# The causal mask moves from a fourth product of each diagonal tile into idle rows of its second and third product

## The reference

```
scores = einsum('bqhd,bkhd->bhqk', q_full, k_full) * softmax_scale
scores = where(causal, scores, finfo.min)      # key after query: hidden
attn   = softmax(scores)
out    = einsum('bhqk,bkhd->bqhd', attn, v)
```

## Time and profile before

| | |
|---|---|
| median of 3 runs | 773.95 us (773.89 to 774.18) |
| the profiled execution | 774.09 us |
| its span | 772.2 us |
| PE busy | 741.6 us, 96% of the span |
| DVE busy | 541.1 us, 70% |
| ACT busy | 326.4 us, 42% |
| POOL busy | 213.3 us, 28% |
| granted TensorE clock | 0.999 |

### The profile page before, as it was taken

The page is one execution under the profiler, slowest core; times in us unless marked ns, Lnnn a source line. Parts: engine busy times, 40 slices in busy tenths (PEclk is TensorE's granted clock), DMA queues, the critical chain, the costliest instruction groups (busy, mean ns, idle before and its releaser), DMA issues.

```text
span 772.2 us, 10622 instructions
## 1 busy us (share of the span) xinstructions
PE 741.6 (96%) x3931; PEld 513.4 (66%) x3931; DVE 541.1 (70%) x803; ACT 326.4 (42%) x499; POOL 213.3 (28%) x198
## 2 busy tenths in 40 slices
PE   3989999999999999999999999999999999999997
PEld 2856666666666666566566666555788888887886
DVE  6867678788788788888888889589695332123432
ACT  4834444545545545545545444444254322222210
POOL 1137624135235235235235211010255000000211
PEclk9999999999999999999999999999999999999999
DMA  8433523403303303303303390350201332200011
GB/s 312 173 76 88 125 56 83 90 9 83 92 8 83 91 8 83 90 10 83 87 12 82 71 346 21 111 191 28 57 26 28 97 79 70 75 11 1 28 42 41
DMA packets 36289, 60.73 MB, mean 79 GB/s; under 512 B 4272, under 2 KB 16560, under 8 KB 34448
## 3 DMA queue, kind: packets, MB, share of 16 engines
q1 hardware_dynamic: 36240, 60.06, 28.0%
HBM read 32.66 MB, written 2.10 MB: 45 GB/s over the span
## 4 chain that ended last, share of the span: by engine, by line
PE 70%; DVE 22%; issue 4%; ACT 2%; DMA 1%; POOL 0%; SPq 0%; DVEq 0%; ACTq 0%; POOLq 0%
PE PS L845 16%; PE PS L862 8%; PE PS L675 8%; DVE PR L1397 6%; PE PS L754 6%; PE PS L735 6%; PE PS L736 6%; PE PS L737 5%; PE PS L809 5%; DVE NMa L1305 4%; PE PS L666 3%; DVE NMd L1310 2%; PE PS L688 2%; PE PS L739 1%; DVE wide L1397 1%
## 5 line engine op out<-in xcount | busy, mean ns | idle before, releaser
L1053 ACT ACTIVATE PR<-PS 128x1024 f32<-128x1024 f32 (+1 forms) x144 | 133.1, 929 | 151.8 <-PE PS L737 127.4
L1305 DVE TENSOR_REDUCE NMa<-PS 128x1 f32<-128x512 f32 (+3 forms) x184 | 116.4, 656 | 34.7 <-PE PS L675 33.1
L675 PE MATMUL PS<-KH,Q 96*128 96x128 f32 (+3 forms) x576 | 131.5, 331 | 7.9 <-DVE NMa L1305 2.9
L675 PEld LDWEIGHTS PS<-KH,Q 96*128 96x128 f32 x576 | 88.2, 190 | 58.4 <-issue 30.4
L735 PE MATMUL PS<-Q,KH 97*128 97x512 f32 x280 | 117.2, 418 | 0.0
L736 PE MATMUL PS<-Q,KL 96*128 96x512 f32 x288 | 115.0, 399 | 0.0
L1397 DVE TENSOR_TENSOR PR<-PR 128x2048 f32<-128x2048 f32 (+3 forms) x56 | 111.7, 1995 | 4.4 <-ACT PR L1053 1.9
L737 PE MATMUL PS<-Q,KH 96*128 96x512 f32 x288 | 113.5, 394 | 0.0
L1640 POOL TENSOR_SCALAR_AFFINE_SELECT diag<-diag 128x512 f32<-128x512 f32 x64 | 46.8, 731 | 204.8 <-ACT diag L998 204.8
L754 PE MATMUL PS<-PR,V 128*32 128x512 f32 (+3 forms) x704 | 70.2, 486 | 0.0
L735 PEld LDWEIGHTS PS<-Q,KH 97*128 97x128 f32 x280 | 53.1, 190 | 22.6 <-issue 13.4
(11 more groups left out here) (191 smaller groups left out, 1127.7 us busy)
## 6 DMA issues: line engine op xcount, KB each, us to landing
Q<-TQ SPq DMA_DIRECT2D x64, 384.0 KB, 5.6
RT<-in_wo SPq DMA_DIRECT2D x4, 1024.0 KB, 4.8
TQ<-in_wo SPq DMA_DIRECT2D x4, 1024.0 KB, 4.8
WI<-in_gate_w SPq DMA_DIRECT2D x10, 256.0 KB, 3.3
WI<-in_up_w SPq DMA_DIRECT2D x10, 256.0 KB, 4.0
DI<-in_down_w SPq DMA_DIRECT2D x10, 256.0 KB, 2.8
PR<-in_wmod_c SPq DMA_DIRECT2D x2, 1024.0 KB, 6.7
x_in<-in_x SPq DMA_DIRECT2D x8, 256.0 KB, 9.1
```

Of the source, the lines that this page charges most:

```text
L675: ins = pe.matmul(bank[:, i * w:(i + 1) * w], M.Q[0:KR, g % 2, 0, qt // 4, h0 + i, qs], M.KH[0:KR, lo:lo + w], start=(i == 0), stop=(i == ...
L1053: act.activation(tiles, banks, ACT.Exp).then_inc(S_.p, 1)
L1305: dve.tensor_reduce(dst, PS[:, bank_of(turn), 0:n * w].rearrange("p (h k) -> p h k", k=w), axis=AX.X, op=ALU.max, negate=True).then_inc(S_ ...
```

## The change

The mask goes into partitions 97 to 127 (and 96, where it is free), which the products left idle. Two small tables of powers of two, one for keys and one for queries, are built on the host (`mask_rows`) so that their product is a very large negative number where the key is after the query and nearly nothing elsewhere. The key rows are written once to the low rows of KL (32 partitions) and KH (31, since row 96 holds the ones), and the query rows to Q high (32 partitions) and Q low (31, since the row of maxima now lies there). For a diagonal unit the second and third product take 128 rows in place of 96 and 97, and the fourth is gone. The products of the first unit of a window now stand in the same order as in the others, and the wait for the maxima is ahead of the third.

The tables are loaded by one new DMA behind the load of WA, and POOL copies them to the product format in the tile `mask_made`, which lies where `diag` is later. Four DMAs, right behind the weights of group 1, spread them over all key tiles and all query tiles of the even parity; two more DMAs in window 0 copy the query rows to the odd parity. ACT's first two diagonal copies wait for the four, PE waits for them ahead of window 0's first unit, and for the two ahead of window 1's.

```
+def mask_levels():
+    sizes = [2] * (MASK_ROWS * 2 - 3) + [3] * 3
+    starts = [sum(sizes[:n]) for n in range(len(sizes))]
+    return list(zip(starts, sizes))
+def mask_rows():
+    k = np.zeros((2, L, P), np.float32)
+    q = np.zeros((2, L, P), np.float32)
+    for n, (start, size) in enumerate(mask_levels()):
+        hide, keep = (30, 45) if size == 2 else (20, 32)
+        row = (n // MASK_ROWS, 1 + n % MASK_ROWS)
+        for i in range(size):
+            q[row + (start + i,)] = -2.0 ** (hide - i * (hide + keep))
+            k[row + (start + 1 + i,)] = 2.0 ** (i * (hide + keep))
+        k[row + (slice(start + size + 1, P),)] = 2.0 ** ((size - 1) * (hide + keep))
...
     def send_maxima(g):
-        sp.dma_start(M.Q[KR:KR + 1, g % 2, 0].rearrange(...)
+        sp.dma_start(M.Q[KR:KR + 1, g % 2, 1].rearrange(...)
+    def send_mask_rows(kind, dst, done):
+        lo = P - dst.shape[0]
+        n = dst.shape[1] // P
+        sp.dma_start(dst.rearrange("p (n q) -> p n q", q=P).bitcast(F32),
+                     M.mask_made[lo:P, kind, :].bitcast(F32).unsqueeze(1).broadcast_to([P - lo, n, P])).then_inc(done, 16)
+    def copy_mask_rows(hl, done):
+        lo = KR + hl
+        sp.dma_start(M.Q[lo:P, 1, hl]..., M.Q[lo:P, 0, hl]...).then_inc(done, 16)
...
     load_weights(1)
+    sp.wait_ge(S_.mm, 1)
+    send_mask_rows(0, M.KL[KR:P, :], S_.mk)
+    send_mask_rows(1, M.KH[KR + 1:P, :], S_.mk)
+    for hl in range(2):
+        send_mask_rows(2 + hl, M.Q[KR + hl:P, 0, hl].rearrange("p f h q -> p (f h q)"), S_.mk)
     sp.wait_ge(S_.one, 1)
     send_queries(0, 0)
...
             send_queries(w + 1, 1)
+        if w == 0:
+            sp.wait_ge(S_.pj, NS)
+            sp.wait_ge(S_.mk, 64)
+            for hl in range(2):
+                copy_mask_rows(hl, S_.mq)
...
-        first = s == 0 and i == 0
-        if not first:
-            pe.matmul(dst, M.KH[0:KR + 1, ks], M.Q[0:KR + 1, w % 2, 0, qb, :, qs], start=True, stop=False)
-        pe.matmul(dst, M.KL[0:KR, ks], M.Q[0:KR, w % 2, 0, qb, :, qs], start=first, stop=False)
-        ins = pe.matmul(dst, M.KH[0:KR, ks], M.Q[0:KR, w % 2, 1, qb, :, qs], start=False, stop=not (diagonal or first))
-        if diagonal:
-            ins = pe.matmul(dst, M.maskb[:], M.identb[:].unsqueeze(1).broadcast_to([P, HG, P]), start=False, stop=not first)
-        if first:
+        if diagonal and s == 0:
+            if w == 0:
+                pe.wait_ge(S_.mk, 64)
+            if w == 1:
+                pe.wait_ge(S_.mq, 32)
+        pe.matmul(dst, M.KH[0:KR, ks], M.Q[0:KR, w % 2, 0, qb, :, qs], start=True, stop=False)
+        rows = P if diagonal else KR
+        pe.matmul(dst, M.KL[0:rows, ks], M.Q[0:rows, w % 2, 0, qb, :, qs], start=False, stop=False)
+        if s == 0 and i == 0:
             pe.wait_ge(S_.nd, 16 * (w + 1))
-            ins = pe.matmul(dst, M.KH[0:KR + 1, ks], M.Q[0:KR + 1, w % 2, 0, qb, :, qs], start=False, stop=True)
+        rows = P if diagonal else KR + 1
+        ins = pe.matmul(dst, M.KH[0:rows, ks], M.Q[0:rows, w % 2, 1, qb, :, qs], start=False, stop=True)
...
     def diagonal_copied(g, k):
+        if g == 0 and qt < 2:
+            act.wait_ge(S_.mk, 64)
...
-    pool.affine_select(out=M.maskb[:], in_=M.maskb[:], compare_op=ALU.is_ge, fill=MASKED, base=0, ...)
+    pool.wait_ge(S_.mr, 16)
+    pool.tensor_copy(M.mask_made[KR:P], M.mask_raw[KR:P]).then_inc(S_.mm, 1)
```

More of the change, by code:

```diff
@@ L21 @@
 KR = 2 * HALF + L
+MASK_ROWS = P - KR - 1
 KD = D // P
@@ L67, in is_diagonal @@
     return PARTS[k][1] == PARTS[k][0] * P
+def mask_levels():
+    sizes = [2] * (MASK_ROWS * 2 - 3) + [3] * 3
+    starts = [sum(sizes[:n]) for n in range(len(sizes))]
+    assert sum(sizes) == P - 1
+    return list(zip(starts, sizes))
[9 more added lines that the diff above has]
+        k[row + (slice(start + size + 1, P),)] = 2.0 ** ((size - 1) * (hide + keep))
+    return np.concatenate([k, q]).transpose(1, 0, 2)
 def softmax_scale():
@@ L151, in __init__ @@
         self.nj, self.nm, self.nd = sem("halves_joined"), sem("maxima_joined"), sem("maxima_sent")
-        self.mask = sem("masks")
+        self.mask = sem("more_constants")
+        self.mr, self.mm, self.mk, self.mq = (
+            sem("mask_rows_loaded"), sem("mask_rows_made"), sem("mask_rows_even_sent"), sem("mask_rows_odd_sent"))
         self.sc, self.p, self.pv = sem("scores"), sem("weights"), sem("values")
@@ L216, in __init__ @@
         self.RT = take("RT", [P, 4, 512])
+        made = self.at
         self.diag = take("diag", [P, 2, HG, P])
@@ L227, in __init__ @@
         self.identb = take("identb", [P, P], BF16)
-        self.maskb = take("maskb", [P, P], BF16)
         self.c_rows = take("c_rows", [P, D])
@@ L233, in __init__ @@
         self.NMj = take("NMj", [P, 2, HG, NS // 2])
+        self.at = made
+        self.mask_raw = take("mask_raw", [P, 2 * 2, P])
+        self.mask_made = take("mask_made", [P, 2 * 2, P], F32R)
+        assert self.at <= loaded
         self.at = wide
@@ L498, in send_maxima @@
         wait_free(sp, ("rows", g))
-        sp.dma_start(M.Q[KR:KR + 1, g % 2, 0].rearrange("p f h (n q) -> p (f h n) q", q=P).bitcast(F32),
+        sp.dma_start(M.Q[KR:KR + 1, g % 2, 1].rearrange("p f h (n q) -> p (f h n) q", q=P).bitcast(F32),
                      M.NM[:].bitcast(F32)).then_inc(S_.nd, 16)
+    def send_mask_rows(kind, dst, done):
[5 more added lines that the diff above has]
+        lo = KR + hl
+        sp.dma_start(M.Q[lo:P, 1, hl].rearrange("p f h q -> p (f h q)").bitcast(F32),
+                     M.Q[lo:P, 0, hl].rearrange("p f h q -> p (f h q)").bitcast(F32)).then_inc(done, 16)
     def load_wo(m):
@@ L524, in sp_program @@
             sp.dma_start(M.WA[:], t["wa"]).then_inc(S_.wa, 16)
+            sp.dma_start(M.mask_raw[KR:P], t["mask_rows"]).then_inc(S_.mr, 16)
         if st == 2:
@@ L718, in keep_busy @@
         for _ in range(times):
-            pe.matmul(PS[:, bank, :], M.maskb[:], M.identb[:].unsqueeze(1).broadcast_to([P, HG, P]), start=True, stop=True)
+            pe.matmul(PS[:, bank, :], M.identb[:], M.identb[:].unsqueeze(1).broadcast_to([P, HG, P]), start=True, stop=True)
     def scores(w, s, i):
@@ L765, in pe_program @@
         if st == 0:
-            pe.wait_ge(S_.mask, 6)
+            pe.wait_ge(S_.mask, 4)
             keep_busy(7, 6)
@@ L1585, in pool_program @@
     pool.memset(M.identb[:], 0.0).then_inc(S_.mask, 1)
-    pool.memset(M.maskb[:], 0.0).then_inc(S_.mask, 1)
     pool.memset(M.NMa[:], -MASKED).then_inc(S_.mask, 1)
     pool.memset(M.NMb[:], -MASKED).then_inc(S_.mask, 1)
-    pool.wait_ge(S_.mask, 2)
+    pool.wait_ge(S_.mask, 1)
     pool.affine_select(out=M.identb[:], in_=M.identb[:], compare_op=ALU.not_equal, fill=1.0, base=0,
                        pattern=[[-1, P]], channel_multiplier=1).then_inc(S_.mask, 1)
-    pool.affine_select(out=M.maskb[:], in_=M.maskb[:], compare_op=ALU.is_ge, fill=MASKED, base=0,
-                       pattern=[[-1, P]], channel_multiplier=1).then_inc(S_.mask, 1)
-    pool.wait_ge(S_.mask, 6)
+    pool.wait_ge(S_.mask, 4)
+    pool.wait_ge(S_.mr, 16)
+    pool.tensor_copy(M.mask_made[KR:P], M.mask_raw[KR:P]).then_inc(S_.mm, 1)
+    pool.wait_ge(S_.mm, 1)
     def keys(st):
```

1 line of the change is left out of this document (added).

## The result

The changed kernel takes 785.12 us (median of 4 runs, 784.76 to 786.67) where the kernel before takes 774.00. The ratio is 1.0147, with a 95% interval from 1.0130 to 1.0165: slower by 1.5%. The forecast was 783.8, from 772 to 798.

The account below looks back on a forecast made before the run. The prediction took PE, busy 96% of the span, and DVE as both near their limit in the windows, with savings read from the chain of waits. 774.1 - 9.8 + 18 + 1.5 = 783.8 us, range 772 to 798.

Parts of the forecast that it names:

- One engine for 31 rows: Mask transfers ahead of the first queries: those of 31 rows go through one DMA engine, which has 38.3 us of packets.
- The delay of 18 us: First stage: queries behind the mask make the first maxima product 16.6 us late, the fourth 20; 18 taken.
- The clock, 1.5: After PE's wait of some 16 us in the first stage, products run at half rate; cost 1.5 us, bounds 0 and 4.
- The gain of 9.8: Over all windows 64 mask products go; 42 on the chain of waits count, at 0.233 us each, saving 9.8 us.
- The maxima's wait: At the product needing the maxima, PE with three masks fewer still arrives 0.64 us after they land; cost 0.
- The copy: In window 0, copying the query rows: 31 rows take 26 us on one engine, hidden before window 1 needs them.
- The start: One 64 KB load behind WA, two POOL instructions fewer and one copy more, covered by POOL's idle time; cost 0.
- The first rival: Mask transfers at the start: the 31 rows are spread after all, nothing is paid; 764.3 us, 759 to 770; chance 0.13.

Follow-up runs that it names:

- e1: Changed kernel with each transfer of 31 rows cut into 15 and 16 rows; 765.32 us, ratio 0.9888 to the kernel before.
- e9: Changed kernel with the 31 rows cut as 29 + 2, in the mask's transfers and the copy; 784.19 us.
- e3: Changed kernel with 66 more filler products on PE ahead of the first maxima product, so PE does not idle there; 785.85 us.
- e5: Changed kernel with the key's 31 rows cut into 15 and 16, the copy cut too, the query's 31 rows left whole; 780.99 us.
- e7: e1 with the old fourth product put back in diagonal units 7, 9, 26 and 30 of each window; 767.08 us.
- e8: e1 with the old fourth product put back in diagonal units 0, 4, 33 and 35 of each window; 772.24 us.
- e6: e1 with the copy in window 0 left as one transfer of 31 rows; 765.64 us.
- e2: Kernel before, fourth products kept, with the mask's tables, transfers and waits added in rows its products don't read; 796.05 us.
- e4: Changed kernel with the four mask transfers, 31 rows still whole, moved ahead of the weights of group 1 on SP; 777.40 us.

## Why the prediction was right

**One engine for 31 rows** was the step on which the sign hung, and it held: 370 packets in 10 us with no other packet moving, and e1 and e9 with the same bytes in other shapes.

**The delay of 18 us** was a little short. Working it again with what was measured: 1320 packets at 27.0 ns instead of 29 are 35.6 us, by which the first queries are there at 34.8 + 2.2 + 35.6 + 1.7 = 74.3. They landed at 75.2 (48.83 + 26.4), where I had 77.0. To the first diagonal copy on ACT, which needs the fourth head, the delay has grown to 18.0 (80.22 against 62.26), because the heads come 1.1 to 1.8 us apart. I expected DVE to catch some of it up; it did not. In the changed kernel's profile the fourth such copy is 21.1 late (93.13 against 72.06), and 19.0 in e3 (91.06), which has the clock for most of the stage. So 19 is the measure of this term without the clock. From medians: 785.12 - 765.32 = 19.8. I had 18 + 1.5 = 19.5. ACT's first and fourth diagonal copy, in the changed kernel and then before:

```profile
80.22 0.60 ACT L1060 ACTIVATE diag<-PS 128x512 f32<-128x512 f32 x1 [20.93 <-PE PS L733]
...
93.13 0.60 ACT L1060 ACTIVATE diag<-PS 128x512 f32<-128x512 f32 x1 [2.14 <-PE PS L733]
```

```profile
62.26 0.60 ACT L998 ACTIVATE diag<-PS 128x512 f32<-128x512 f32 x1 [2.34 <-PE PS L675]
...
72.06 0.60 ACT L998 ACTIVATE diag<-PS 128x512 f32<-128x512 f32 x1 [2.14 <-PE PS L675]
```

**The clock, 1.5.** PE did fall to a granted 0.53 after its idle stretch, where I had only an indirect sign of it. The filler's mean from 80 to 93 shows it, in the changed kernel and then in e3:

```profile
L777 PE MATMUL PS<-identb 128*128 128x512 bf16 x7 | 4.0, 576 | 0.0
```

```profile
L777 PE MATMUL PS<-identb 128*128 128x512 bf16 x9 | 4.0, 449 | 0.0
```

In the profiled execution that is 2.1 us, and in the trace of e5 0.3; in the medians of e3 it can't be seen. The term stays between 0 and 2.

**The gain of 9.8** was 9.0 by the profile and 9.1 by the medians of e1's set. The turns cut the 42 products that I counted into 4, five times 4, 8 and 10 behind the last turn; at 0.233 us these are 0.9, 4.7, 1.9 and 2.3, and measured were 0.8, 4.6 (0.87 to 0.99 a window), 1.0 and 2.6. So the count failed in one place, the stretch ahead of the last turn. There the chain held 7.5 us of DVE's work before and holds 12.2 now, 2.5 of it in adds (`wide`) that weren't on it: about half of what PE gave up went into waiting for DVE. e7 and e8 confirm the reading of windows 1 to 5 unit by unit: the ones off the chain cost nothing. That all 42 would count in full was not covered by what I had looked at, since I had checked DVE only at the start of one window.

**The maxima's wait** is 0.4 us, once, in window 0. In the other windows it is none, as the margin of 0.64 said.

**The copy** was 26 us by the estimate, hidden. It was issued at 118.6, the engines leave their single-engine pattern at about 141, 22 later, and nobody waited for it or for the queries of group 2 behind it. e6 confirms it.

**The start** cost nothing to be seen; outside the span 0.5 us are added (786.67 - 784.3 against 774.09 - 772.2), in e1's as well. All kernels without the old mask tile and its products have it (2.2 to 2.7 us outside the span); those that keep them do not (before, e2, e7 and e8, 1.8 to 1.9). What causes it is open.

**The first rival**, an even spread, gave 764.3. It was false for this kernel, and right as a price: e1, which makes it true, runs at 765.3. Its own working was too light, though. I had the mask's packets done by 44; spread, they take from 36.5 to 46.7, since 16 engines at once move these runs at 125 GB/s and not 16 times 19. The margin to the first queries is 2.3 us and not five.

**What I had wrong in the mechanism**: I had the one engine's share of the queries come late and took the other shares to pass. In fact SP itself stands still. It cost little here, as a transfer lands with its last share anyhow, but in e4 it decided.

**How much was luck.** Little. The sum was 1.3 us under the median, with a delay too small by about 1, a gain too large by 0.8, and a clock term that is not settled. These two misses add up; the clock term, where it is nearer 0.3 than 1.5, takes a part of them back. What was at stake was the choice of one engine over an even spread, which lie 19.5 us apart.

## What to carry to other kernels

Look at the number of rows of a transfer before its bytes: 31 or 29 rows moved at the rate of one DMA engine, and cutting them 15 + 16 or 21 + 10 was worth 19 to 20 us, for two more instructions at the start and one in window 0. A saving on PE is priced by the chain of waits place by place: here products on the chain were worth their full 0.23 us in windows 1 to 5, and those off it nothing. Being on the chain is no guarantee, since another engine may take over: in the stretch ahead of the last turn eight of them gave half. And a gain and a loss at different places of a program are best told apart by a milestone that recurs, as the turn of the maxima does here, and by one run for each side.

## What was not expected of the hardware

- A DMA instruction on SP lasted 21.5 us by itself where the median of its line is 1.4 (and 27.05 in e4 where the same load takes 0.33 before), with a transfer ahead of it in the queue that had far to go on one engine. With it everything behind it stood, also transfers that share no data with it. From 60 to 70 us all sixteen engines together moved what one can.
- One packet of 512 bytes each 27.0 ns on one engine (19 GB/s), but 125 GB/s over 16 engines, 8 for each. Runs of 16 KB, in the copy, go at 25 GB/s on one engine.
- PE had no work for 15.3 us. In that stretch the granted TensorE clock fell from 1.00 to 0.50 (1.2 GHz; it reads 0.81 from 64 to 66 us), and it stayed at 0.50 until 88, although PE was busy for 13.3 of the 14.6 us from 75.4 on; from 90 it was 1.00. In e5, whose first maxima product comes 3.7 us earlier, it was back some 8 us earlier.
